# One branch around all of TensorE's rounds, and the output weight's argument on GpSimd, in an RWKV and SwiGLU layer

## The chip, the cores and the metric

The kernel runs on one core of a Trainium2 chip. The metric is the device time of one execution in microseconds (us). The time before is the median of three runs, 326.41 us (324.96 to 333.9). A core has five engines that run their own instruction streams and wait for each other by semaphores: TensorE (PE; its weight loads are PEld), VectorE (DVE), ScalarE (ACT), GpSimd (POOL) and SyncE (SP, which only issues transfers here).

## The reference

The input is `x`, 4096 rows of 256 numbers. The layer is an RWKV attention and a SwiGLU feed-forward, each followed by a residual and a layer norm:

```python
xk = x*mix_k + xx*(1-mix_k)        # xx: x shifted by one row; the same for v and r
k, v, sr = xk@Wk.T, xv@Wv.T, sigmoid(xr@Wr.T)
# per channel, over the rows in order, w = -exp(time_decay), u = time_first
q = max(pp, u+k);  y = (exp(pp-q)*aa + exp(u+k-q)*v) / (exp(pp-q)*bb + exp(u+k-q))
q2 = max(pp+w, k); aa, bb, pp = exp(pp+w-q2)*aa + exp(k-q2)*v, exp(pp+w-q2)*bb + exp(k-q2), q2
x1  = layernorm(x + (sr*y)@Wo.T)
out = layernorm(x1 + (silu(x1@(wg/127).T) * (x1@(wu/127).T)) @ (wd/127).T)
```

`wg`, `wu` and `wd` are int32 matrices (768 hidden columns) with values from -127 to 127.

## The kernel before, in words

The 4096 rows are cut into nine chunks (`NC`): seven of 512 rows, and one of 256 at either end. Channels lie on the partitions, as two halves `h` of 128. Round `j` does the attention of chunk `j`, the feed-forward of chunk `j-1`, and prepares chunks `j+1` and `j+2`. Each engine has its order written out by hand: rounds 0, 1, 2, 7 and 8 stand by themselves, rounds 3 to 6 in a loop (`Fori`), two rounds in a pass on TensorE, ScalarE and GpSimd, one on VectorE. So a loop of TensorE makes two passes.

In a round TensorE computes gate and up of chunk `j-1` (L1012, six tiles of 128 hidden columns), `down` (L1035), then `attention_out` of chunk `j` (L980), the projections K and V of chunk `j+1` (L970), the transposes of `x1` (L989) and the projection R (L970). The matrices of the feed-forward exist in two forms: values that TensorE's fast format (`f32r`) holds exactly, used when all weights are below 4096 in size, and full float32, used when not. Which of the two is decided at run time: a flag `wide` is made by VectorE in round 0 and loaded into a register of TensorE (L1105), and each of the rounds 1 to 8, and the last `ffn_products`, has an `If` with both forms written out (L1060). With the inputs of the reference the first form always runs, and at its end TensorE jumps over the second, to `attention_out`.

The recurrence is done with a running maximum `pmax` (L616) and `gap = k - pmax` (L623). Three exponentials follow for each half of a chunk. Their arguments are made by VectorE in `exp_args` (L633) from `gap`: `IN_NEW` and `IN_OLD` with the decay, and `OUT`, the weight of the current row in the output, as `min(gap + time_first, 30)`. ScalarE takes the exponentials (`weight`, L414). It waits for VectorE's counter `args_ready`, in the order of the arguments. The scans over the rows (L650, L662) begin when all three weights of a half are there.

In a steady round VectorE's order after the scans is: products of gate and up (L758), the low parts of the last two hidden tiles (L766), gating (L696), `divide` (L705, writes `rwkv`), the residual of the feed-forward (L774) and its statistics, the residual of the attention (L725) and its statistics (L712, L717), the running maxima, the gaps, the arguments of half 0, `shift_rows2` (L781), `IN_NEW` and `IN_OLD` of half 1, the low parts of `x1` (L746), `OUT` of half 1, and then the next round's scans.

GpSimd's order in a round is: low parts of four hidden tiles (L348) with the two halves of the numerator (L340) between them, then, once `rwkv` is written, the differences `dx` (L327) and the sums `mix` (L333) of chunk `j+2`. Then it waits for the next round's first hidden tile.

Of the kernel before, what the change touches and what calls it, by code (L numbers as in the profile page):

```python
# [14 lines left out]
def rwkv_swiglu_kernel(nc: bass.Bass, xT: bass.AP, x: bass.AP, params: bass.AP, wk: bass.AP, wv: bass.AP,  # L15
# [4 lines left out]
    ALU = mybir.AluOpType  # L20
# [29 lines left out]
    with ctx:  # L50
# [131 lines left out]
        args_ready = sem("args_ready")  # L182
        wts_ready = sem("wts_ready")
# [138 lines left out]
        def _(pool):  # L322
# [19 lines left out]

            def low_part(c, m):
# [16 lines left out]
            def round_(j, s, ffn, ahead):  # L360
# [11 lines left out]
                if ahead:  # L372
                    pool.wait_ge(rwkv_ready, j + 1)
                    diffs(j + 2)
                    mix_chunk(j + 2, s)

# [4 lines left out]
            for h in range(CH):  # L381
                pool.wait_ge(r0_scaled, h + 1)
                nc.gpsimd.tensor_tensor(mix0[:, R, h, :], mix0[:, R, h, :], xt0[:, h, 0:steps(0)],
                                        ALU.add).then_inc(r0_mixed, 1)
            diffs(1)
            mix_chunk(1, 1)
            pool.wait_ge(wd_in, 16)
            nc.gpsimd.tensor_copy(wd_r[:, :, :], wd_i[:, :, :]).then_inc(wd_ready, 1)
            diffs(2)
# [11 lines left out]
            with pool.Fori(3, NC - 2, 2) as j:  # L401
                round_(j, 1, True, True)
                round_(j + 1, 0, True, True)
# [6 lines left out]
        def _(sc):  # L410
            def weight(c, i, h):
                sc.wait_ge(args_ready, c * (NW * CH) + (h * NW + i + 1))
# [190 lines left out]
        def _(dve):  # L603
# [22 lines left out]
            def exp_args(c, h, which=range(NW)):  # L626
# [4 lines left out]
                for i in which:  # L631
                    s = par[:, FIRST, h:h + 1] if i == OUT else decay[:, h:h + 1]
                    nc.vector.tensor_scalar(wts[:, i, h, 0:n], gap[:, h, 0:n], s, CAP if i == OUT else 0.0, ALU.add,  # L633
# [150 lines left out]
            def round_(j, ffn, nxt):  # L784
# [40 lines left out]
                if first(j):  # L825
# [4 lines left out]
                    exp_args(1, 1, [IN_NEW, IN_OLD])  # L830
                    wide_flag()
                    norm_rows(0, x1, res1, mv1, rstd1, rstd1_ready, x1_ready, halved(0))
                    exp_args(1, 1, [OUT])
# [19 lines left out]
                exp_args(j + 1, 1, (IN_NEW, IN_OLD))  # L853
                x1_low(j, 0)
                x1_low(j, 1)
                exp_args(j + 1, 1, [OUT])
# [82 lines left out]
        def _(pe):  # L939
# [118 lines left out]
            def round_(j, s, ffn, nxt):  # L1058
                if ffn:
                    with pe.If(any_wide == 0):  # L1060
                        ffn_products(j, False)
                    with pe.Else():
                        ffn_products(j, True)
# [45 lines left out]
            round_(1, 0, True, True)  # L1109
            round_(2, 1, True, True)  # L1110
            with pe.Fori(3, NC - 2, 2) as j:
                round_(j, 0, True, True)
                round_(j + 1, 1, True, True)
            round_(NC - 2, 0, True, True)
            round_(NC - 1, 1, True, False)
            with pe.If(any_wide == 0):
                ffn_products(NC, False)
# [30 lines left out]
```

## Time and profile before

| | |
|---|---|
| median of 3 runs | 326.41 us (324.96, 326.41, 333.9) |
| the profiled execution | 325.1 us, of which the span of the instructions is 323.3 us |
| mean granted clock of TensorE | 0.954 of full speed |
| busy share: PE, PEld, DVE, ACT, POOL | 87%, 64%, 84%, 67%, 46% |
| instructions on PE, DVE, ACT, POOL | 1250, 484, 386, 123 |
| the chain that ended last, by engine | DVE 32%, PE 30%, issue 17%, ACT 15%, DMA 3% |

A busy share is an average over the whole span. "Issue" in the chain is time in which an engine waited for nothing that the profile shows. Semaphore, register and branch instructions are not counted as busy. The time of the profiled execution is 1.8 us more than its span.

### The profile page before, as it was taken

The page shows a single profiled execution, that of the slowest core. Times are in us where ns is not written, and L with a number is a line of the kernel's source. Part 1 is how long each engine was busy: PE and PEld are TensorE (multiplying, and loading weights), DVE is VectorE, ACT ScalarE, POOL GpSimd, SP SyncE. Part 2 cuts the span into 40 slices and gives each one's busy share as a digit, 9 for nine tenths or more (in the row PEclk, how much of TensorE's full clock was granted, in tenths as well). Part 3 has the DMA queues.
Part 4 walks back from the last instruction along what each step waited for, and adds up shares of the span by engine and source line. Part 5 has one row for each costly group of instructions (what it writes and reads, how often), then busy time and mean ns, then how long its engine had stood idle before and what let it go on. Part 6 is the DMA issues. An engine that isn't in the chain of part 4 may idle for free.

```text
span 323.3 us, 4411 instructions
## 1 busy us (share of the span) xinstructions
PE 280.9 (87%) x1250; PEld 205.6 (64%) x1250; DVE 272.6 (84%) x484; ACT 218.0 (67%) x386; POOL 148.8 (46%) x123
## 2 busy tenths in 40 slices
PE   7878869908997999599997999999989998999892
PEld 5624756505885468465885568846785588868782
DVE  4999798629985999669986899899989998989664
ACT  3587767069764688529884498569855986299275
POOL 2564255491569019560378208570759056006030
PEclk9979799976997999989997999999999999999998
DMA  7802200402000301012010401020012001101002
GB/s 256 296 0 65 68 1 2 132 0 65 32 3 3 130 3 65 2 30 102 2 65 5 130 0 65 0 74 23 6 58 65 0 1 67 36 0 65 2 6 99
DMA packets 13531, 16.38 MB, mean 51 GB/s; under 512 B 704, under 2 KB 11200, under 8 KB 13504
## 3 DMA queue, kind: packets, MB, share of 16 engines
q1 hardware_dynamic: 12816, 15.48, 14.5%
q10 hardware_dynamic: 688, 0.53, 0.5%
q8 instruction: 18, 0.29, 0.4%
q14 instruction: 9, 0.07, 0.1%
HBM read 11.81 MB, written 4.19 MB: 50 GB/s over the span
## 4 chain that ended last, share of the span: by engine, by line
DVE 32%; PE 30%; issue 17%; ACT 15%; DMA 3%; DVEq 1%; POOL 1%; SPq 0%; ACTq 0%; POOLq 0%
PE bank_b L980 7%; PE bank_b L1012 6%; PE bank_a L1012 6%; DVE hid L758 4%; DVE wts L633 3%; ACT L512 3%; PE bank_c L970 3%; DVE stats L712 3%; DVE pmax L616 3%; DVE state L662 3%; ACT den L452 2%; ACT x L437 2%; ACT den L458 2%; DVE res L725 2%; DVE rwkv L705 2%
## 5 line engine op out<-in xcount | busy, mean ns | idle before, releaser
L348 POOL TENSOR_TENSOR hlo<-hid,hhi 128x512 fp32r<-128x512 f32 (+1 forms) x36 | 47.5, 1321 | 123.2 <-ACT hhi L496 123.2
L333 POOL TENSOR_TENSOR mix<-mix,xt 128x512 f32<-128x512 f32 x48 | 56.7, 1213 | 13.0 <-ACT mix L422 13.0
L1035 PE MATMUL bank_a<-wd_r,hhi 128*128 128x256 f32 x192 | 47.3, 287 | 4.6 <-DVE hlo L766 4.6
L422 ACT ACTIVATE mix<-dx,par 128x512 f32<-128x512 f32 x48 | 31.2, 710 | 27.0 <-POOL dx L327 26.9
L1035 PE MATMUL bank_a<-wd_r,hlo 128*128 128x256 f32 x192 | 45.6, 279 | 0.0
L980 PE MATMUL bank_b<-woT,rwkv 128*128 128x256 f32 x128 | 34.9, 432 | 8.6 <-issue 7.6
L1035 PEld LDWEIGHTS bank_a<-wd_r,hhi 128*128 128x128 f32 x192 | 36.0, 188 | 7.8 <-issue 7.0
L496 ACT ACTIVATE hhi<-hid 128x512 fp32r<-128x512 f32 (+1 forms) x54 | 31.1, 578 | 10.6 <-DVE hid L758 10.6
L980 PEld LDWEIGHTS bank_b<-woT,rwkv 128*128 128x128 f32 x128 | 27.2, 218 | 14.7 <-issue 8.8
L1035 PEld LDWEIGHTS bank_a<-wd_r,hlo 128*128 128x128 f32 x192 | 36.0, 188 | 0.3 <-issue 0.2
L414 ACT ACTIVATE wts<-wts 128x512 f32<-128x512 f32 (+1 forms) x54 | 27.9, 578 | 8.3 <-DVE wts L633 8.3
L1012 PE MATMUL bank_a<-x1hi,wg_r 128*128 128x512 f32 (+1 forms) x96 | 31.9, 412 | 1.6 <-ACT act L488 1.0
L488 ACT ACTIVATE act<-bank_a 128x512 f32<-128x512 f32 (+1 forms) x48 | 27.3, 568 | 6.6 <-PE bank_a L1012 6.1
L758 DVE TENSOR_TENSOR hid<-bank_b,act 128x512 f32<-128x512 f32 (+1 forms) x48 | 30.6, 642 | 1.3 <-PE bank_b L1012 0.8
L970 PE MATMUL bank_d<-mix,wvT 128*128 128x512 f32 (+1 forms) x64 | 28.9, 596 | 2.3 <-POOL mix L333 2.3
L1012 PE MATMUL bank_b<-x1hi,wu_r 128*128 128x512 f32 (+1 forms) x96 | 29.2, 385 | 1.6 <-DVE hid L758 1.6
L1012 PE MATMUL bank_a<-x1lo,wg_r 128*128 128x512 f32 (+1 forms) x96 | 29.0, 382 | 0.1
L1012 PE MATMUL bank_b<-x1lo,wu_r 128*128 128x512 f32 (+1 forms) x96 | 28.8, 381 | 0.0
L970 PE MATMUL bank_c<-mix,wrT 128*128 128x512 f32 (+1 forms) x64 | 28.7, 591 | 0.0
L327 POOL TENSOR_TENSOR dx<-xt 128x512 f32<-128x512 f32 x16 | 16.5, 1054 | 25.3 <-DVE rwkv L705 16.1
L970 PE MATMUL bank_a<-mix,wkT 128*128 128x512 f32 (+1 forms) x64 | 27.2, 567 | 1.1 <-POOL mix L333 1.1
L472 ACT ACTIVATE lnv<-mv,eps 128x4 f32<-128x4 f32 (+1 forms) x18 | 5.2, 289 | 30.5 <-DVE mv L717 30.5
(103 smaller groups left out, 571.7 us busy)
## 6 DMA issues: line engine op xcount, KB each, us to landing
xt<-xT SPq DMA_DIRECT2D x7, 513.0 KB, 4.7
xrow<-x SPq DMA_DIRECT2D x7, 512.0 KB, 3.8
out<-y SPq DMA_DIRECT2D x6, 512.0 KB, 2.8
wg_i<-wg SPq DMA_DIRECT2D x1, 768.0 KB, 7.7
wu_i<-wu SPq DMA_DIRECT2D x1, 768.0 KB, 9.1
wd_i<-wd SPq DMA_DIRECT2D x1, 768.0 KB, 10.4
out<-y SPq DMA_DIRECT2D x3, 256.0 KB, 2.1
xt<-xT SPq DMA_DIRECT2D x2, 257.0 KB, 3.0
```

The costliest lines, as they stand in the source:

```text
L327: nc.gpsimd.tensor_tensor(dx[:, h, 0:n], xt[:, h, 1:n + 1], xt[:, h, 0:n], ALU.subtract).then_inc(dx_ready, 1)
L333: nc.gpsimd.tensor_tensor(mix[:, s, i, h, 0:n], mix[:, s, i, h, 0:n], xt[:, h, 0:n], ALU.add).then_inc(mixed, 1)
L348: nc.gpsimd.tensor_tensor(hlo[:, m, 0:n], hid[:, m % NH, 0:n], hhi[:, m, 0:n].bitcast(f32), ALU.subtract).then_inc(hlo_ready, 1)
L414: nc.scalar.activation(wts[:, i, h, 0:n], wts[:, i, h, 0:n], ACT.Exp, scale=-1.0 if i == IN_OLD else 1.0).then_inc(wts_ready, 1)
L422: nc.scalar.activation(mix[:, s, i, h, 0:n], dx[:, h, 0:n], ACT.Copy, scale=par[:, MIX + i, h:h + 1]).then_inc(dx_scaled, 1)
L488: nc.scalar.activation(act[:, m % 2, 0:n], gate_bank(c)[:, m % 2, 0:n], ACT.Silu, scale=SCALE).then_inc(act_ready, 1)
L496: nc.scalar.activation(hhi[:, m, 0:n], hid[:, m % NH, 0:n], ACT.Copy).then_inc(hhi_ready, 1)
L758: nc.vector.tensor_tensor(hid[:, m % NH, 0:n], up_bank(c)[:, m % 2, 0:n], act[:, m % 2, 0:n], ALU.mult).then_inc(hid_ready, 1)
L970: mm = nc.tensor.matmul(bank[:, d, 0:n], w[:, h, d * P:(d + 1) * P], mixed_x[:, i, h, 0:n], start=(h == 0), stop=(h == CH - 1))
L980: mm = nc.tensor.matmul(attn[:, q, :], rwkv[:, h, q * P:(q + 1) * P], woT[:, h, :], start=(h == 0), stop=(h == CH - 1))
L1012: mm = nc.tensor.matmul(bank[:, m % 2, 0:steps(c)], w[:, h, m * P:(m + 1) * P], xp, start=(h == 0 and part is x1hi), stop=(h == CH - 1 and ...
L1035: mm = nc.tensor.matmul(ffn[:, q, :], hp.bitcast(f32) if full else hp, w[:, m, :], start=(m == 0 and q % 2 == 0 and part is hhi), stop=(m ...
```

## The change

Three things are changed.

TensorE: the `If` on `any_wide` no longer stands in each round but once, around everything from round 1 to the end, with the whole sequence of rounds (and its loop) written out in either branch.

The `OUT` argument is made by GpSimd, in a new function `out_arg`, with a semaphore of its own; VectorE's `exp_args` makes only `IN_NEW` and `IN_OLD`. ScalarE's order of the exponentials is the same; for `OUT` it waits for the new semaphore.

GpSimd: the loop over rounds 3 to 6 is written out as four rounds.

```diff
+            def out_arg(c, h):
+                pool.wait_ge(gap_ready, c * CH + (h + 1))
+                n = steps(c)
+                nc.gpsimd.tensor_scalar(wts[:, OUT, h, 0:n], gap[:, h, 0:n], par[:, FIRST, h:h + 1], CAP, ALU.add,
+                                        ALU.min).then_inc(out_arg_ready, 1)
...
                     mix_chunk(j + 2, s)
+                if not last(j):
+                    out_arg(j + 1, 0)
+                    out_arg(j + 1, 1)
...
+            pool.wait_ge(par_in, 16)
+            out_arg(0, 0)
             diffs(1)
+            out_arg(0, 1)
             mix_chunk(1, 1)
             pool.wait_ge(wd_in, 16)
             nc.gpsimd.tensor_copy(wd_r[:, :, :], wd_i[:, :, :]).then_inc(wd_ready, 1)
+            out_arg(1, 0)
+            out_arg(1, 1)
             diffs(2)
...
-            with pool.Fori(3, NC - 2, 2) as j:
-                round_(j, 1, True, True)
-                round_(j + 1, 0, True, True)
+            for j in range(3, NC - 2):
+                round_(j, j % 2, True, True)
...
             def weight(c, i, h):
-                sc.wait_ge(args_ready, c * (NW * CH) + (h * NW + i + 1))
+                if i == OUT:
+                    sc.wait_ge(out_arg_ready, c * CH + (h + 1))
+                else:
+                    sc.wait_ge(args_ready, c * (2 * CH) + (h * 2 + i + 1))
...
-            def exp_args(c, h, which=range(NW)):
+            def exp_args(c, h):
...
-                for i in which:
-                    s = par[:, FIRST, h:h + 1] if i == OUT else decay[:, h:h + 1]
-                    nc.vector.tensor_scalar(wts[:, i, h, 0:n], gap[:, h, 0:n], s, CAP if i == OUT else 0.0, ALU.add,
+                for i in (IN_NEW, IN_OLD):
+                    nc.vector.tensor_scalar(wts[:, i, h, 0:n], gap[:, h, 0:n], decay[:, h:h + 1], 0.0, ALU.add,
                                             ALU.max if i == IN_OLD else ALU.min).then_inc(args_ready, 1)
...
-                exp_args(j + 1, 1, (IN_NEW, IN_OLD))
+                exp_args(j + 1, 1)
                 x1_low(j, 0)
                 x1_low(j, 1)
-                exp_args(j + 1, 1, [OUT])
...
-            def round_(j, s, ffn, nxt):
+            def round_(j, s, ffn, nxt, full=False):
                 if ffn:
-                    with pe.If(any_wide == 0):
-                        ffn_products(j, False)
-                    with pe.Else():
-                        ffn_products(j, True)
+                    ffn_products(j, full)
...
+            def rounds(full):
+                round_(1, 0, True, True, full)
+                round_(2, 1, True, True, full)
+                with pe.Fori(3, NC - 2, 2) as j:
+                    round_(j, 0, True, True, full)
+                    round_(j + 1, 1, True, True, full)
+                round_(NC - 2, 0, True, True, full)
+                round_(NC - 1, 1, True, False, full)
+                ffn_products(NC, full)
+
             with pe.If(any_wide == 0):
-                ffn_products(NC, False)
+                rounds(False)
             with pe.Else():
-                ffn_products(NC, True)
+                rounds(True)
```

How the instructions stand in a row shows at three places. First TensorE in round 2, from the last products of `down` to `attention_out`, before (the names `wg_r`, `wd_r` are the exact form, `wg_i`, `wd_i` the full float32 form):

```order
L1035 MATMUL bank_a<-wd_r,hlo 128x256
L1060 UNCONDITIONAL_BRANCH
L1012 MATMUL bank_a<-x1hi,wg_i 128x512 x2
L1012 MATMUL bank_a<-x1lo,wg_i 128x512 x2
...
L1035 MATMUL bank_a<-wd_i,hlo 128x256
L1062 UNCONDITIONAL_BRANCH
L980 MATMUL bank_b<-woT,rwkv 128x256 x8
L970 MATMUL bank_a<-mix,wkT 128x512 x4
```

The same place with the change:

```order
L1049 MATMUL bank_a<-wd_r,hhi 128x256
L1049 MATMUL bank_a<-wd_r,hlo 128x256
L1049 MATMUL bank_a<-wd_r,hhi 128x256
L1049 MATMUL bank_a<-wd_r,hlo 128x256
L994 MATMUL bank_b<-woT,rwkv 128x256 x8
L984 MATMUL bank_a<-mix,wkT 128x512 x4
L984 MATMUL bank_d<-mix,wvT 128x512 x4
```

The second form no longer lies between `down` and `attention_out`, and no branch is there.

Second, GpSimd at the end of the loop's first round and the start of its second, before (`ISA` and `REGISTER_ALU` set the values that a wait compares with):

```order
L331 REGISTER_ALU
L333 TENSOR_TENSOR mix<-mix,xt 128x512
L344 ISA
L348 TENSOR_TENSOR hlo<-hid,hhi 128x512
L344 REGISTER_ALU
L348 TENSOR_TENSOR hlo<-hid,hhi 128x512
L344 REGISTER_ALU
L348 TENSOR_TENSOR hlo<-hid,hhi 128x512
```

And with the change, at the end of a round and the start of the next:

```order
L328 TENSOR_TENSOR dx<-xt 128x512 x2
L334 TENSOR_TENSOR mix<-mix,xt 128x512 x6
L347 TENSOR_SCALAR wts<-gap,par 128x512 x2
L355 TENSOR_TENSOR hlo<-hid,hhi 128x512 x3
L341 TENSOR_TENSOR num<-kv,state 128x512
```

The two arguments of `OUT` stand behind the sums of `mix` and ahead of the next round's low parts.

Third, VectorE at the end of a steady round, from the gaps on, before:

```order
L623 TENSOR_TENSOR gap<-bank_a,pmax 128x512 x2
L633 TENSOR_SCALAR wts<-gap,decay 128x512 x2
L633 TENSOR_SCALAR wts<-gap,par 128x512
L781 SCALAR_TENSOR_TENSOR shift<-mv,rstd 128x4
L633 TENSOR_SCALAR wts<-gap,decay 128x512 x2
L746 TENSOR_TENSOR x1lo<-bank_b,x1hi 128x512 x2
L633 TENSOR_SCALAR wts<-gap,par 128x512
```

And with the change:

```order
L640 TENSOR_TENSOR gap<-bank_a,pmax 128x512 x2
L649 TENSOR_SCALAR wts<-gap,decay 128x512 x2
L797 SCALAR_TENSOR_TENSOR shift<-mv,rstd 128x4
L649 TENSOR_SCALAR wts<-gap,decay 128x512 x2
L762 TENSOR_TENSOR x1lo<-bank_b,x1hi 128x512 x2
```

One instruction between the pairs of arguments is gone, and one behind the low parts of `x1`.

## Rows read from the trace of the kernel before

**Rows 1.** Windows between `rwkv`s: start:end, length, busy PE PEld DVE ACT POOL, PEclk, DMA, GB/s.
```profile
95.48:132.25 36.77, 33.68 (x144) 24.36 (x144) 31.38 (x55) 25.34 (x43) 18.15 (x14) 0.95 0.13 45
132.25:169.48 37.23, 33.76 (x144) 24.33 (x144) 31.19 (x56) 25.35 (x43) 18.04 (x14) 0.95 0.14 44
169.48:206.34 36.86, 33.77 (x144) 24.33 (x144) 31.39 (x55) 25.33 (x43) 18.12 (x14) 0.95 0.13 44
206.34:240.03 33.69, 32.12 (x144) 22.90 (x144) 31.87 (x56) 25.11 (x43) 18.57 (x14) 1.00 0.13 39
240.03:273.69 33.66, 32.21 (x144) 23.04 (x144) 32.02 (x56) 25.10 (x43) 18.54 (x14) 1.00 0.10 32
```

**Rows 2.** The chain that ended last: its pieces between `down` and `attention_out` (start, us, what).
```profile
96.86 2.38 issue
...
133.66 2.85 issue
...
170.89 2.39 issue
...
305.40 1.10 issue
```

**Rows 3.** Timeline of PE: `attention_out` of rounds 4 and 5 (start, us, instruction, idle before).
```profile
173.28 5.40 PE L980 MATMUL bank_b<-woT,rwkv 128*128 128x256 f32 x16 [2.39 <-issue]
...
207.69 3.72 PE L980 MATMUL bank_b<-woT,rwkv 128*128 128x256 f32 x16
```

**Rows 4.** The window of round 4's `attention_out`, same columns as the windows above.
```profile
173.28:178.68 5.40, 5.40 (x17) 4.48 (x18) 1.44 (x3) 2.82 (x5) 5.40 (x6) 0.68 0.02 5
```

**Rows 5.** DMA queues from 95 to 105 us: packets, MB, share.
```profile
q8 instruction: 2, 0.03, 1.3%
```

**Rows 6.** DMA queues from 175 to 260 us, the only queue with packets.
```profile
q1 hardware_dynamic: 3184, 3.41, 12.7%
```

**Rows 7.** Timeline of VectorE and ScalarE at the end of round 5.
```profile
217.73 1.25 DVE L623 TENSOR_TENSOR gap<-bank_a,pmax 128x512 f32<-128x512 f32 x2
218.91 0.86 DVE L633 TENSOR_SCALAR wts<-gap,decay 128x512 f32<-128x512 f32 x2
219.70 0.47 DVE L633 TENSOR_SCALAR wts<-gap,par 128x512 f32<-128x512 f32 x1
220.10 0.15 DVE L781 SCALAR_TENSOR_TENSOR shift<-mv,rstd 128x4 f32<-128x4 f32 x1
...
221.08 1.29 DVE L746 TENSOR_TENSOR x1lo<-bank_b,x1hi 128x512 fp32r<-128x512 f32 x2
222.29 0.48 DVE L633 TENSOR_SCALAR wts<-gap,par 128x512 f32<-128x512 f32 x1
...
221.43 2.19 ACT L414 ACTIVATE wts<-wts 128x512 f32<-128x512 f32 x4
```

**Rows 8.** Timeline of GpSimd: the next round's first low part, and its idle time before.
```profile
228.01 1.46 POOL L348 TENSOR_TENSOR hlo<-hid,hhi 128x512 fp32r<-128x512 f32 x1 [11.41 <-ACT hhi L496]
```

**Rows 9.** Groups on GpSimd, shapes apart: count | busy us, mean ns of one.
```profile
L340 POOL TENSOR_TENSOR num<-kv,state 128x512 f32<-128x512 f32 x14 | 25.4, 1811 | 0.0
L327 POOL TENSOR_TENSOR dx<-xt 128x512 f32<-128x512 f32 x16 | 16.5, 1054 | 25.3 <-DVE rwkv L705 16.1 <-DMA xt<-xT 9.2
L388 POOL CAST wd_r<-wd_i 128x1536 fp32r<-128x1536 int32 x1 | 1.5, 1460 | 0.0
L379 POOL TENSOR_SCALAR_AFFINE_SELECT ident<-ident 128x128 f32<-128x128 f32 x1 | 0.3, 292 | 0.2 <-POOL ident L377 0.2
```

**Rows 10.** Timeline of the first 30 us: arguments on VectorE beside work on GpSimd.
```profile
13.48 1.18 DVE L633 TENSOR_SCALAR wts<-gap,par 128x256 f32<-128x256 f32 x1
28.28 2.32 POOL L327 TENSOR_TENSOR dx<-xt 128x512 f32<-128x512 f32 x2 [2.50 <-DMA xt<-xT]
29.62 1.26 DVE L633 TENSOR_SCALAR wts<-gap,par 128x512 f32<-128x512 f32 x1
```

**Rows 11.** Timeline of VectorE in the last round: the rows that TensorE transposes.
```profile
305.28 0.74 DVE L732 TENSOR_SCALAR xt<-res,mv,rstd 128x256 f32<-128x256 f32 x2 [0.67 <-ACT rstd L474]
```

More of the change, by code:

```diff
@@ L182, in rwkv_swiglu_kernel @@
         args_ready = sem("args_ready")
+        out_arg_ready = sem("out_arg_ready")
         wts_ready = sem("wts_ready")
@@ L829, in round_ @@
                     range_flag()
-                    exp_args(1, 1, [IN_NEW, IN_OLD])
+                    exp_args(1, 1)
                     wide_flag()
                     norm_rows(0, x1, res1, mv1, rstd1, rstd1_ready, x1_ready, halved(0))
-                    exp_args(1, 1, [OUT])
                     x1_low(0, 0)
@@ L1108, in _ @@
             pe.wait_ge(wd_ready, 1)
[L1109 to L1115, printed above, removed]
+            def rounds(full):
[7 more added lines that the diff above has]
+                ffn_products(NC, full)
             with pe.If(any_wide == 0):
-                ffn_products(NC, False)
+                rounds(False)
             with pe.Else():
-                ffn_products(NC, True)
+                rounds(True)
 def kernel(**inputs):
```

## The prediction

> **What bounds the kernel now.** I cut the span into windows first, from one `rwkv` to the next, for rounds 2 to 7 [rows 1]. Three periods take 36.77, 37.23 and 36.86 us, the next two 33.69 and 33.66 us, with the same counts of matmuls. A round can therefore run in 33.7 us, and three do not: 3.09 + 3.55 + 3.18 = 9.8 us more.
>
> The chain of waits says where. In each of the three, TensorE has a piece of "issue" between the last product of `down` and `attention_out`: 2.38, 2.85 and 2.39 us, and one of 1.10 us in the last round [rows 2]. `rwkv` had been written before that time was over, so no data were missing. In round 5 the same 16 matmuls follow `down` at once [rows 3]. The second effect is the clock: they take 5.40 us behind the pause and 3.72 us without it [rows 3], at a granted clock of 0.68 [rows 4] against 1.00 in the whole of that round [rows 1]. Pause and slow clock make TensorE 2.4 + 1.7 = 4.1 us late. Of that VectorE, which has the feed-forward's residual to do meanwhile, hides 0.9; 3.2 us stay in the period.
>
> What stands at this place in the program is the jump over the full float32 form. The queues support it: from 95 to 105 us, around the first pause, the instruction queue q8 moves two packets [rows 5]; from 175 to 260 us, the loop's second pass and a little more, only the data queue moves anything [rows 6]. I read the pause as the fetch of code at a jump's target that is not at hand.
>
> In an undisturbed round VectorE bounds: 31.9 of 33.7 us busy [rows 1], and dense from the gaps into the scans [rows 7].
>
> **The change, part by part.** *The branch.* It removes the jump from rounds 1 to 8 and the pause with it. Rounds 2, 3 and 4 should take what 5 and 6 take: 9.8 us less. What is late next is what bounds rounds 5 and 6 already, so this is not an extrapolation. The order shows no second copy of the products in TensorE's path any more. One jump over the whole second sequence remains, behind all of TensorE's work, where VectorE's last norm and the store end the kernel: nothing. The loop's jump back stays; before, it cost nothing, since round 5 needed no fetch [rows 6] though its body held both forms. Now it is shorter.
>
> *The last round.* The 1.10 us piece goes [rows 2]. Four warming matmuls and the transposes behind it move forward; their input comes from VectorE, at 305.28 + 0.74 = 306.02 [rows 11], 0.5 us before the pause's end, and the warming matmuls run ahead of it. I take 1.0 us, bounds 0.5 and 1.1.
>
> *`OUT` off VectorE.* Two instructions per steady round go, at 219.70 and 222.29 [rows 7]. Each occupies VectorE for 0.40 us, the step from 219.70 to the next one's start at 220.10. The first gains nothing ahead of `x1`'s low parts, which start just when ScalarE has written their input; the second is directly ahead of the next scans and gains 0.4.
>
> *`OUT` on GpSimd.* The trace has no such instruction. GpSimd has done its sums at 228.01 - 11.41 = 216.6 and is then idle until the next round's first low part [rows 8], so its own time is covered; ScalarE takes `OUT` of half 0 only at 221.43 [rows 7], 3 us after its gap. The price is paid by VectorE. Beside work of GpSimd one argument took 1.18 us (256 wide) and 1.26 us (512 wide) [rows 10] against 0.47 alone [rows 7]: it ended 0.28 us after GpSimd's instruction did, so it had waited for it. Now GpSimd starts on half 0 at about 218.5, exactly when VectorE comes to its arguments. Call one such instruction D. The nearest rows: the cast, one input, 1460/1536 = 0.95 ns an element, so 0.49 us and some 0.2 us of fixed time for 512 elements (an affine select of 128 takes 0.29); two inputs take 1.05 us, contended 1.81 [rows 9]. I take D = 0.7, by the row with one input; ends 0.5 and 1.8. With 0.7: GpSimd 218.5 to 219.2, VectorE's first argument until 219.6, GpSimd's half 1 until 220.3, VectorE's second until 220.7, against 219.70 before. The next pair and `shift_rows2` follow at 220.7, and the low parts start at 221.5 instead of 221.08: +0.45, less the 0.40 behind them. That is +0.05 us a round, and 2(D - 0.7) more for another D. Over seven rounds: +0.3, taken as 0, with ends -2.5 (D = 0.5) and +15.7 (D = 1.8).
>
> The Trainium skill gives a lower price (GPSIMD Engine Reference, section "Elementwise — side-by-side cycle accounting": a loop with one or two operations runs at about 1.03 cycles an element), an estimate of 0.44 us for 512 elements; by it the seven rounds would give back some 3 us rather than nothing, and the time would be near 310.5. No run here shows it.
>
> *The start.* VectorE is the chain up to 25 us. The two `OUT` instructions of 1.18 and 1.26 us there [rows 10] go, 2.4 us; but GpSimd now waits for a gap ahead of `dx`, and the collisions shift rather than vanish. I take 1.5, bounds 0 and 2.8 (with the two shorter ones of half 0). It survives: the load of chunk 3 waits for a residual of round 1 and moves along.
>
> *GpSimd's loop written out.* It is idle for 11 us of a round; nothing.
>
> **Sum.** 9.8 + 1.0 + 1.5 + 0 = 12.3 us. Against the profiled execution (325.1 us, of which 323.3 is the span) that gives 312.8. That execution lies between the lowest and the middle run of three; the median is 1.3 us above it, so the same sum against the median gives 314.1. I say 313.5.
>
> **The rivals.**
> *A. The stall moves.* The rows do not say why the jumps of rounds 1 and 7 cost nothing, so how much code is at hand is inferred. If TensorE's jump back to round 5 misses now, one period pays 3.2 us again: 316.7. Against it stands that the second pass needed no fetch [rows 6]. Chance 0.08. The Trainium skill speaks for this rival (Runtime: NRT & Kernel Launch, section "Instruction fetch mechanics": only two blocks of code are held, and a taken branch outside them stalls); by that rule the second pass before should have fetched too, and the trace disagrees, with no packet on q8 in 85 us.
> *B. The port eats it.* D near 1.3, as with two inputs: 7 x 2 x 0.6 = 8.4 us, giving 321.9. For it: GpSimd's arithmetic in this trace is never under 1.05 us at this width. Against: one input only. Chance 0.10; at about D = 1.1 the result passes from "faster by 2%" to "within 2%".
> *C. The change doesn't do what it says:* the pause belongs not to the jump but to `attention_out` itself, and stays. Only 1.5 us come: 325. Against: round 5 has no pause at the same instruction. Chance 0.05.
> *D. Slower.* GpSimd needs 2.3 us or more for this form (a minimum behind an addition with a per-partition operand, which no row shows). VectorE's arguments then wait for two such instructions in every round: 7 x 3.2 = 22 us, and the start's 1.5 are lost: 337.5. It decides from D = 2.1 on. Against: the longest arithmetic of this width, contended, is 1.8 us on average [rows 9]. Chance 0.03.
>
> **The numbers.** The forecast has 0.74. Its own range goes from 325.1 - 9.8 - 1.1 - 2.8 - 2.5 = 308.9 to 318 (nothing at the start, D = 0.9). With A and most of B inside, the range is 308.5 to 321. This kernel's measurement tells 2%, 6.5 us, from no change: faster means below 319.9. Faster: 0.74 + 0.08 + half of B (0.04) = 0.86. Within 2%: rest of B, and C, 0.11. Slower: 0.03.
>
> **What would show it.** All periods near 33.7 us, no "issue" ahead of `attention_out`, its 16 matmuls at 3.7 us with the clock at full speed in every round. GpSimd's new instruction at about 0.7 us, right behind the gaps; VectorE's first two arguments stretched to about 1.8 us together, scans no later than before. In the last round, transposes 1 us sooner. It is wrong if a pause stands at another place of TensorE's stream, if D is over 1.1 us, or if rounds 5 and 6 are themselves longer than 34.5 us.

## The result and the profile after

The changed kernel takes 311.18 us (median of 4 runs, 310.65 to 311.65). Of the kernel before there were then four runs, 324.96, 326.41, 333.9 and one of 458.12. The ratio of the times, taken with the first two of these, is 0.9554, with a 95% interval of 0.9509 to 0.9599: 4.5% faster. The profiled execution took 311.22 us (span 309.4) against 325.1 (span 323.3): 13.9 us less. The forecast was 313.5 us, with 12.3 us for the profiled execution.

The windows of the changed kernel from one `rwkv` to the next come first, rounds 1 to 6 of it; columns as in [rows 1], which hold rounds 2 to 6:

```profile
51.72:93.51 41.79, 30.64 (x134) 22.33 (x132) 29.40 (x47) 26.59 (x45) 28.33 (x20) 0.88 0.13 45
93.51:126.17 32.66, 31.94 (x144) 23.16 (x144) 31.14 (x54) 25.31 (x43) 22.61 (x16) 1.00 0.16 49
126.17:159.86 33.69, 32.22 (x144) 22.91 (x144) 31.82 (x53) 25.20 (x43) 22.90 (x16) 1.00 0.15 48
159.86:193.56 33.70, 32.40 (x144) 23.05 (x144) 31.83 (x53) 25.21 (x43) 22.90 (x16) 1.00 0.16 47
193.56:227.25 33.69, 32.40 (x144) 23.08 (x144) 31.81 (x53) 25.21 (x43) 22.92 (x16) 1.00 0.13 39
227.25:259.81 32.56, 31.94 (x144) 23.15 (x144) 30.90 (x53) 25.23 (x43) 18.61 (x16) 1.00 0.10 33
```

The three long periods of [rows 1] are 4.11, 3.54 and 3.16 us shorter, 10.8 together; the fourth is as before (33.69); the fifth is 1.0 shorter (its end in [rows 1] was read 0.08 us late: `rwkv` of round 7 starts at 273.61, so it was 33.58). `rwkv` of round 1 is written at 51.72 instead of 54.20, and the period after it is 0.5 longer (41.79 for 41.28). From the last `rwkv` to the end nothing changes (23.35 us for 23.47). 2.5 - 0.5 + 10.8 + 1.0 + 0.1 are the 13.9 us.

TensorE's `attention_out` of round 5 (timeline; start, us, instruction), and the instruction queue over the whole span, first of the kernel before, then of the changed one:

```profile
194.92 3.72 PE L994 MATMUL bank_b<-woT,rwkv 128*128 128x256 f32 x16
```

```profile
q8 instruction: 18, 0.29, 0.4%
```

```profile
q8 instruction: 10, 0.16, 0.2%
```

No idle time stands ahead of the 16 matmuls in any of the rounds 2 to 6, and the clock is at full speed in all their periods (PEclk 1.00 above, where [rows 1] had 0.95 three times). So both effects that [rows 3] and [rows 4] show, the pause and the slow clock behind it, are gone.

The end of round 5 on VectorE, GpSimd and ScalarE, which answers to [rows 7] and [rows 8]:

```profile
204.86 1.25 DVE L640 TENSOR_TENSOR gap<-bank_a,pmax 128x512 f32<-128x512 f32 x2
205.62 4.43 POOL L347 TENSOR_SCALAR wts<-gap,par 128x512 f32<-128x512 f32 x2 [1.89 <-DVE gap L640]
...
206.04 0.94 DVE L649 TENSOR_SCALAR wts<-gap,decay 128x512 f32<-128x512 f32 x2
...
206.97 1.22 DVE L649 TENSOR_SCALAR wts<-gap,decay 128x512 f32<-128x512 f32 x2
208.28 1.29 DVE L762 TENSOR_TENSOR x1lo<-bank_b,x1hi 128x512 fp32r<-128x512 f32 x2
208.62 2.18 ACT L431 ACTIVATE wts<-wts 128x512 f32<-128x512 f32 x4
209.49 0.58 DVE L659 COPY state<-state 128x4 f32<-128x4 f32 x1
```

One argument takes GpSimd 2.2 us, not 0.7. And yet VectorE is hardly held: its four arguments take 0.94 and 1.22 us where they took 0.86 and 0.87, the copy of the state 0.58 where it took 0.16. That is 0.85 us more, about what the two instructions taken from it gave (0.8). ScalarE gets the last argument at 205.62 + 4.43 = 210.05, and the last of its four exponentials begins at 210.2: the margin is 0.2 us.

### The profile page after: what moved, and what is told of

It is laid out like the page before. It is cut to its first block, busy times and chain, and to the rows that moved or that the text cites. A ratio compares the mean times of both kernels' runs of the same rounds, so it can differ in the third digit from the quotient of the medians.

```text
span 309.4 us, 4331 instructions
## 1 busy us (share of the span) xinstructions
PE 273.7 (88%) x1250; PEld 199.5 (64%) x1250; DVE 267.7 (87%) x466; ACT 217.7 (70%) x386; POOL 181.9 (59%) x141
## 4 chain that ended last, share of the span: by engine, by line
PE 41%; DVE 22%; ACT 17%; issue 10%; POOL 4%; DMA 2%; DVEq 1%; SPq 0%; ACTq 0%; POOLq 0%
PE bank_a L1026 10%; PE bank_b L1026 10%; PE bank_c L984 7%; PE bank_b L994 4%; ACT L529 3%; DVE stats L728 3%; ACT x L454 3%; ACT den L469 3%; ACT den L475 3%; PE bank_b L1003 2%; DVE rwkv L721 2%; PE bank_d L984 2%; PE bank_a L984 2%; POOL wts L347 2%; DVE hid L774 2%
## 5 line engine op out<-in xcount | busy, mean ns | idle before, releaser
L355 POOL TENSOR_TENSOR hlo<-hid,hhi 128x512 fp32r<-128x512 f32 (+1 forms) x36 | 50.3, 1399 | 59.6 <-ACT hhi L513 59.5
L334 POOL TENSOR_TENSOR mix<-mix,xt 128x512 f32<-128x512 f32 (+1 forms) x48 | 53.5, 1148 | 6.6 <-ACT mix L439 6.6
L347 POOL TENSOR_SCALAR wts<-gap,par 128x512 f32<-128x512 f32 (+1 forms) x18 | 35.4, 1968 | 25.5 <-DVE gap L640 24.6
L984 PE MATMUL bank_a<-mix,wkT 128*128 128x512 f32 (+1 forms) x64 | 30.0, 615 | 5.3 <-POOL mix L334 5.3
L994 PE MATMUL bank_b<-woT,rwkv 128*128 128x256 f32 x128 | 29.9, 385 | 0.9 <-DVE rwkv L721 0.9
L328 POOL TENSOR_TENSOR dx<-xt 128x512 f32<-128x512 f32 (+1 forms) x16 | 15.7, 1001 | 21.7 <-DVE rwkv L721 15.7
L994 PEld LDWEIGHTS bank_b<-woT,rwkv 128*128 128x128 f32 x128 | 23.7, 190 | 5.4 <-DVE rwkv L721 1.4
L984 PE MATMUL bank_d<-mix,wvT 128*128 128x512 f32 (+1 forms) x64 | 27.1, 566 | 0.0
```

Of the source, the lines that this page charges most:

```text
L334: nc.gpsimd.tensor_tensor(mix[:, s, i, h, 0:n], mix[:, s, i, h, 0:n], xt[:, h, 0:n], ALU.add).then_inc(mixed, 1)
L347: nc.gpsimd.tensor_scalar(wts[:, OUT, h, 0:n], gap[:, h, 0:n], par[:, FIRST, h:h + 1], CAP, ALU.add, ALU.min).then_inc(out_arg_ready, 1)
L355: nc.gpsimd.tensor_tensor(hlo[:, m, 0:n], hid[:, m % NH, 0:n], hhi[:, m, 0:n].bitcast(f32), ALU.subtract).then_inc(hlo_ready, 1)
L984: mm = nc.tensor.matmul(bank[:, d, 0:n], w[:, h, d * P:(d + 1) * P], mixed_x[:, i, h, 0:n], start=(h == 0), stop=(h == CH - 1))
L994: mm = nc.tensor.matmul(attn[:, q, :], rwkv[:, h, q * P:(q + 1) * P], woT[:, h, :], start=(h == 0), stop=(h == CH - 1))
```

## The experiments

The references for all are the changed kernel (311.18 us) and the kernel before. A ratio is to the kernel before as it ran beside the experiment, with its 95% interval. The median of the kernel before was then 329.6, 331.4 and 326.6 us, while the runs of each other kernel lie within 3 us; so I compare the kernels' own medians, and periods. A "profiled" time is that of the one run whose trace is read.

### The branch alone

`rounds(full)` and the single `If` as in the change; VectorE's and GpSimd's parts as before.

> Only TensorE's branch is moved around all rounds; VectorE makes all three arguments and GpSimd has its loop, as before. Theory: the jump was the cause of the pauses. Rounds 3, 4 and 5 (from one rwkv to the next) fall from 36.8 to 37.2 us to 33.7 (or 32.7 where VectorE's carry of the maximum slips between two instructions of GpSimd), nothing else changes, the start least of all: rwkv of round 1 at 54.2 us as before, period 6 to 7 at 33.7. Profiled time 325.1 - 9.8 = 315.3 us, to 314 if one period gives 1 us more. Rival (the pause belongs to attention_out, and what the change gained came from the argument moved): time near 325, pauses of 2.4 us stay.

314.6 us (313.63 to 315.03), ratio 0.9546 (0.9465 to 0.9628); profiled 314.68. Its windows for rounds 1 to 4 and 6:

```profile
54.11:95.67 41.56, 30.75 (x134) 22.39 (x132) 30.70 (x50) 26.84 (x45) 23.15 (x18) 0.88 0.14 45
95.67:128.32 32.65, 31.95 (x144) 23.16 (x144) 31.18 (x55) 25.34 (x43) 18.15 (x14) 1.00 0.16 49
128.32:162.00 33.68, 32.30 (x144) 23.05 (x144) 31.86 (x55) 25.12 (x43) 18.55 (x14) 1.00 0.16 47
162.00:195.70 33.70, 32.30 (x144) 23.05 (x144) 31.87 (x55) 25.13 (x43) 18.48 (x14) 1.00 0.15 47
...
229.40:263.04 33.64, 32.23 (x144) 23.07 (x144) 31.99 (x56) 25.13 (x43) 18.59 (x14) 1.00 0.11 31
```

The steady periods are those of the changed kernel to 0.02 us, with VectorE's two instructions still in place. The branch gave all of the gain there. Of the other 3.5 us of the change, most lie in the start (54.11 for 51.72) and in round 6 (33.64 for 32.56).

### The argument alone

```diff
-                    ffn_products(j, full)
+                    with pe.If(any_wide == 0):
+                        ffn_products(j, False)
+                    with pe.Else():
+                        ffn_products(j, True)
...
-                rounds(False)
+                ffn_products(NC, False)
```

The changed kernel with TensorE's branch back in every round.

> Only the output weight's argument is moved to GpSimd, with GpSimd's loop over rounds 3 to 6 written out; TensorE keeps its branch in every round. Theory: the pauses stay in rounds 2, 3 and 4 (2.4 to 2.9 us each). The start gains the 2.5 us that rwkv of round 1 gained in the changed kernel, less 0.5 in the next period; steady rounds are within 0.1 us of before, although one argument takes GpSimd 2.2 us; the round before chunk 8 gains 1.1 from the loop written out. 325.1 - 2.0 - 1.1 = 322.0 us, bounds 321 and 324. Rival (GpSimd's 2.2 us block VectorE's arguments, and it was the branch that paid for that): steady rounds longer by 1 us or more, the time 325 or above.

325.67 us (324.44 to 327.27), ratio 0.9895 (0.9805 to 0.9985): above the expected bounds (321 to 324) and within the rival's "325 or above", but not by the rival's cause, since no steady round became longer. The start and round 6 gained as expected. What was not expected is on TensorE's weight loads (timeline, last bracket the idle time before):

```profile
170.29 1.98 PEld L994 LDWEIGHTS bank_b<-woT,rwkv 128*128 128x128 f32 x7 [2.58 <-issue]
...
273.59 0.50 PEld L994 LDWEIGHTS bank_b<-woT,rwkv 128*128 128x128 f32 x2 [2.88 <-issue]
```

A fourth pause stands in round 7, with the same instructions on TensorE as before, and makes the period to the last `rwkv` 30.5 us instead of 26.2. The instruction queue shows what differs. Here a packet of code stands at 271.0 us, just behind the last product of `down` (it begins at 270.6). In the kernel before one stands at 271.2, when `down` still waited for VectorE, until 273.8, for its last eight products, and no pause followed. Why it comes earlier there with the same instructions stays open. Round 5, which has no pause, takes 33.70 us, as without the move.

The pause in round 2 parts the two effects, pause and clock (timeline of TensorE, and the window of these matmuls):

```profile
97.63 3.69 PE L994 MATMUL bank_b<-woT,rwkv 128*128 128x256 f32 x16 [2.51 <-issue]
```

```profile
97.63:101.32 3.69, 3.69 (x17) 3.28 (x18) 1.45 (x3) 2.62 (x5) 3.69 (x4) 1.00 0.02 4
```

The clock did not fall behind this pause, and the period is 35.47 us, where the next two, with clocks of 0.70 and 0.68 in the same 16 matmuls, take 37.33 and 36.75. And that although its copy of the carry took 1.02 us, where theirs took 0.17.

### No distance, and the jump at another place

First the kernel before without the full float32 form, which these inputs never take:

```diff
                     with pe.If(any_wide == 0):
                         ffn_products(j, False)
-                    with pe.Else():
-                        ffn_products(j, True)
...
```

The `Else` of the last `ffn_products` goes too.

> The kernel before, with the branch in each round, but without the full float32 form: nothing stands in the Else (left out is the form for weights of 4096 and more, which these inputs never take). Theory (the pause is the fetch of code at a jump's target that is not at hand): compare and branch remain, the distance is gone, so the pauses go too: no issue ahead of attention_out, periods 3, 4 and 5 at 33.7 or 32.7 us, the time that of the branch-only kernel, 314.6 (profiled 314 to 316). Rival (branching itself costs, whatever its distance): pauses of 2.4 us stay in rounds 2, 3 and 4, time near 325.

313.16 us (312.94 to 313.28), ratio 0.943 (0.9358 to 0.9501). Its first three long periods are 32.63, 33.69 and 33.69 us. Nine compares and branches remain and cost nothing that can be seen; it is the distance that cost. The 1.4 us less than with one branch stand at the end: from the last `rwkv` to the end of the span it is 22.15 us here and 23.54 there (see the experiment on the end of the span).

Then the kernel before with the forms exchanged, here and in the last `ffn_products`, so that the jump stands at the round's start:

```diff
-                    with pe.If(any_wide == 0):
-                        ffn_products(j, False)
+                    with pe.If(any_wide == 1):
+                        ffn_products(j, True)
                     with pe.Else():
-                        ffn_products(j, True)
+                        ffn_products(j, False)
```

> The kernel before with the two forms exchanged in the text: the full float32 form stands first and is jumped over at the round's start, ahead of gate and up; behind down nothing is jumped over. The distance is the same. Theory: the fetch is needed as often, but it now falls where the 8 matmuls of the projection R (3.4 us) have already been handed to TensorE, which works on them while the code comes. So no pause is seen ahead of attention_out, and at most 0.5 us ahead of gate and up: 315 to 317 us. Rival (a pause costs the same wherever it stands): a piece of issue of about 2.4 us ahead of the first gate product in three rounds, time 322 to 326.

314.43 us (312.27 to 315.08), ratio 0.9453 (0.9372 to 0.9534): about the time with one branch, by the exchange of two blocks of text. It is not free throughout: `rwkv` of round 1 comes 0.7 us later than with one branch, and rounds 1 and 2 are 0.4 us longer each, while the end, which here has no jump, is 1.4 us shorter. The queue fetches as often as before. The page's line on it, the longest idle time of the weight loads ahead of a gate product, and the windows of rounds 2 and 3:

```profile
q8 instruction: 18, 0.29, 0.4%
```

```profile
113.04 0.30 PEld L1012 LDWEIGHTS bank_a<-x1hi,wg_r 128*128 128x128 f32 x2 [0.94 <-issue]
```

```profile
96.77:129.79 33.02, 32.20 (x144) 23.05 (x144) 31.54 (x56) 25.33 (x43) 18.15 (x14) 1.00 0.16 49
129.79:163.47 33.68, 32.30 (x144) 22.95 (x144) 31.86 (x56) 25.11 (x43) 18.55 (x14) 1.00 0.17 48
```

18 packets, and 0.94 us of idle time once on the weight loads (0.1 us on the matmuls). What was 2.4 to 2.9 us behind `down` is hidden behind the projection R, as the times of the packets show:

```profile
109.34 3.60 PE L970 MATMUL bank_c<-mix,wrT 128*128 128x512 f32 x8
113.05 0.73 PE L1012 MATMUL bank_a<-x1hi,wg_r 128*128 128x512 f32 x2
```

The round's packet is at 110.1 us, and the gate product comes 2.9 us later, while the 3.6 us of matmuls run. In the kernel before the packets of rounds 2, 3 and 4 are at 96.6, 133.4 and 170.7, within 0.3 us of the last product of `down`, and `attention_out` follows 2.6, 3.1 and 2.6 us later with nothing in between. My bound of 0.5 us held for the matmuls, not for the weight loads.

### GpSimd's loop written out

```diff
-            with pool.Fori(3, NC - 2, 2) as j:
-                round_(j, 1, True, True)
-                round_(j + 1, 0, True, True)
+            for j in range(3, NC - 2):
+                round_(j, j % 2, True, True)
```

The branch alone, and this.

> The branch moved, and GpSimd's loop written out, with all arguments on VectorE. It differs from the kernel with the branch alone only in GpSimd's loop. Theory: written out, round 6 knows that chunk 8 has 256 rows, so the differences and sums for it take 256 columns instead of 512: GpSimd's sums end some 3 us earlier there, before VectorE copies the carried maximum, which then takes 0.2 us instead of 1.0. Period 6 to 7 falls from 33.7 to 32.6 us, all others as with the branch alone: 1.1 us less than that kernel. Rival (a written-out loop costs or gives nothing but code): no period changes, the same time as the branch alone.

The sums of `mix` for chunk 8, first in the kernel with the branch alone, then written out:

```profile
232.78 6.88 POOL L333 TENSOR_TENSOR mix<-mix,xt 128x512 f32<-128x512 f32 x6
```

```profile
232.99 3.90 POOL L333 TENSOR_TENSOR mix<-mix,xt 128x256 f32<-128x256 f32 x6 [0.26 <-ACT mix L421]
```

In the loop the chunk's number is a register, and `steps(c)` gives 512 for the last chunk too. Written out, it gives 256, the period falls from 33.64 to 32.56 us, and no other steady period moves by more than 0.1. The time does not show it: 314.34 us (313.94 to 314.78) against 314.6, where 1.1 less was expected. In this kernel's profile `rwkv` of round 1 was 1.3 us later (55.38 for 54.11), with the same code there; of its other runs there is no trace.

### What the GpSimd instruction costs, and whom

The changed kernel with each argument made twice:

```diff
+                nc.gpsimd.tensor_scalar(spare[:, 0:n], gap[:, h, 0:n], par[:, FIRST, h:h + 1], CAP, ALU.add,
+                                        ALU.min).then_inc(spare_ready, 1)
+                pool.wait_ge(spare_ready, c * CH + (h + 1))
```

> The changed kernel, in which GpSimd makes each of its arguments twice, first into a spare tile, then where it belongs, so 9 us of such instructions in a steady round instead of 4.4. Theory (GpSimd's instruction does not hold VectorE for its length; only short overlaps cost): VectorE's arguments and scans lengthen by under 0.5 us a round, but ScalarE takes OUT of half 0 some 2 us late and of half 1 4 us late, and the scans wait for that: 2 to 4 us a round, time 325 to 338. What tells the theories apart is the length of VectorE's four arguments: 2.2 us together now. Rival (the port is held for the whole instruction): they stretch to 4 us or more.

341.43 us (340.55 to 341.93), ratio 1.0279 (1.0199 to 1.0359), 30 us more than the changed kernel; the steady period is 37.59 us, 3.9 more. The end of its round 5, VectorE and ScalarE:

```profile
228.08 0.94 DVE L654 TENSOR_SCALAR wts<-gap,decay 128x512 f32<-128x512 f32 x2
...
229.01 1.22 DVE L654 TENSOR_SCALAR wts<-gap,decay 128x512 f32<-128x512 f32 x2
...
236.29 0.63 ACT L436 ACTIVATE wts<-wts 128x512 f32<-128x512 f32 x1 [2.50 <-POOL wts L352]
...
236.95 1.28 DVE L671 TENSOR_TENSOR_SCAN state<-wts,state 128x512 f32<-128x512 f32 x1 [2.31 <-ACT wts L436]
```

VectorE's arguments take the same 0.94 and 1.22 us with GpSimd busy beside them all the time: it is not held for an instruction's length. The loss is the plain wait: ScalarE for the argument, VectorE's scan for ScalarE. The expected 325 to 338 us were too few, since the start (6.4 us) and round 1 (4.0) pay too.

To see what makes it slow, the argument was replaced (the output weight is then not the reference's): half 0 is one operation with the per-partition operand, half 1 two operations with constants.

```diff
+                if h == 0:
+                    nc.gpsimd.tensor_scalar(wts[:, OUT, h, 0:n], gap[:, h, 0:n], par[:, FIRST, h:h + 1], None,
+                                            ALU.min).then_inc(out_arg_ready, 1)
+                else:
+                    nc.gpsimd.tensor_scalar(wts[:, OUT, h, 0:n], gap[:, h, 0:n], 0.5, CAP, ALU.add,
+                                            ALU.min).then_inc(out_arg_ready, 1)
```

> The changed kernel with other arguments for the output weight, so that GpSimd's time for them can be told apart (the weight computed is not the reference's): half 0 is one operation, a minimum with the per-partition operand; half 1 is two operations, an addition and a minimum, with constants. In the changed kernel both operations with the per-partition operand take 2.0 us uncontended, where the forecast took 0.7. Theory 1: the second operation costs, so half 0 takes 0.6 to 0.8 us and half 1 about 2.0. Theory 2: the per-partition operand costs, so half 0 takes about 2 and half 1 0.7. Theory 3: both halves take 1.5 to 2.0, the instruction is slow in any form. The time changes by under 1 us in all of them, 310 to 311.5.

Groups on GpSimd (count | busy us, mean ns of one):

```profile
L351 POOL TENSOR_SCALAR wts<-gap 128x512 f32<-128x512 f32 x7 | 13.8, 1970 | 0.6
L348 POOL TENSOR_SCALAR wts<-gap,par 128x512 f32<-128x512 f32 x7 | 12.5, 1787 | 11.4 <-DVE gap L644 11.4
```

1.97 and 1.79 us: neither the second operation nor the operand alone makes the difference to the forecast's 0.7 us. Theory 3 held; one operation with a constant was not run. The time is that of a single run, 309.6 us.

### The end of the span

The changed kernel with the two sequences exchanged (`If(any_wide == 1): rounds(True)`, `Else: rounds(False)`), so that TensorE jumps at the start and falls through at the end.

> The changed kernel with the two sequences of rounds exchanged: TensorE jumps over the full float32 sequence at the start of round 1 and falls through at the end. Theory: the changed kernel loses 1.2 us at its end (3.3 us from the last store's issue to the end of the span, 2.1 before) because TensorE's last jump fetches blocks of code on the same DMA engines as the last store; with the exchange this comes back, and one fetch of 2.4 us stands ahead of round 1's gate products, where the warming matmuls hide part: 310.5 us, bounds 309 and 312.5. Rival (the end of the span varies for another reason): 3.3 us at the end stay, time 311 to 313.5.

311.03 us (310.55 to 311.51), ratio 0.9372 (0.9301 to 0.9444) against a slower set of runs of before, so no different from 311.18. The issue of the last store, before, changed, exchanged (spans 323.3, 309.4 and 308.6 us):

```profile
320.84 0.37 SPq L287 DMA_DIRECT2D out<-mix  x1
```

```profile
305.72 0.37 SPq L288 DMA_DIRECT2D out<-mix  x1
```

```profile
306.18 0.37 SPq L288 DMA_DIRECT2D out<-mix  x1
```

From that issue's end to the end of the span: 2.1, 3.3 and 2.0 us. So the changed kernel's last jump costs 1.2 us at the very end, and the exchange takes it back. All traces agree: the eight in which TensorE jumps over the whole second sequence at its end have one packet of code in the last 5 us of the span and 2.8 to 3.8 us from the store's issue to the end; the other six have no such packet and 2.0 to 2.1 us. In the changed kernel the packet is at 305.2 us, half a microsecond ahead of the store. That the two share a DMA engine is likely, but was not shown.

The jump at the start does not come for nothing: TensorE's first gate product of round 1 is 3.5 us late behind it (it begins at 40.16, with 3.50 us of idle time before it), but these products wait for other engines later, and `rwkv` of round 1 comes only 0.7 us later (52.44 for 51.72).

### What holds VectorE: a small copy

The periods of 32.6 and 33.7 us differ in one instruction. The carry of the running maximum (2 elements a partition) in rounds 2 and 5 of the changed kernel:

```profile
100.17 0.22 DVE L625 COPY pmax<-pmax 128x2 f32<-128x2 f32 x1
...
200.49 1.00 DVE L625 COPY pmax<-pmax 128x2 f32<-128x2 f32 x1
```

In round 5 the copy ends at 201.49, with the GpSimd sum that runs from 200.36 to 201.46; in round 2 it starts 0.2 us before the end of one. The statistics behind it lead to `x1`. The kernel before has both too, in a long round (4) and in a short one (5):

```profile
180.24 0.17 DVE L608 COPY pmax<-pmax 128x2 f32<-128x2 f32 x1
...
213.26 1.09 DVE L608 COPY pmax<-pmax 128x2 f32<-128x2 f32 x1
```

In round 4 GpSimd had done its sums at 179.71, since the pause of TensorE holds VectorE up and not GpSimd; in round 5 they last to 216.60. The edit:

```diff
-                nc.vector.tensor_copy(pmax[:, :, 0:1], pmax[:, :, n:n + 1]).then_inc(pmax_carried, 1)
+                nc.vector.tensor_reduce(pmax[:, :, 0], pmax[:, :, n:n + 1], mybir.AxisListType.X,
+                                        ALU.max).then_inc(pmax_carried, 1)
```

> The changed kernel, with one instruction of VectorE in another form: the last column of the running maximum is carried by a reduction over one element instead of a copy. Theory: in steady rounds this copy (1.0 us for 2 elements a partition; 0.17 to 0.22 where GpSimd is idle or between two instructions) waits for GpSimd's sum that runs beside it, and it lies on the chain to x1, since the statistics are aggregated behind it; a reduction is not held. Periods 3 to 6 fall from 33.7 us to about 32.8, those of 2 to 3 and 6 to 7 (32.7, 32.6) stay; 3 x 0.85 = 2.6 us less, 308.6 against 311.2. Rival 1: the wait passes to the next instruction on the ports, shift_rows1 (two inputs in SBUF), and the time stays. Rival 2: the reduction waits as well: same durations as the copy.

308.11 us (306.81 to 309.33), ratio 0.9344 (0.9258 to 0.943). The same place, and the windows of rounds 3 to 5:

```profile
199.07 0.16 DVE L625 TENSOR_REDUCE pmax<-pmax 128x2 f32<-128x2 f32 x1
```

```profile
126.84:159.49 32.65, 32.02 (x144) 23.17 (x144) 30.80 (x53) 25.35 (x43) 22.41 (x16) 1.00 0.16 49
159.49:192.15 32.66, 32.02 (x144) 23.16 (x144) 30.81 (x54) 25.34 (x43) 22.44 (x16) 1.00 0.16 49
192.15:224.80 32.65, 32.01 (x144) 23.18 (x144) 30.81 (x53) 25.34 (x43) 22.44 (x16) 1.00 0.13 40
```

All steady periods are now 32.6 to 32.7 us, and TensorE is busy for 32.0 of them. The Trainium skill (SBUF — State Buffer, section "Who interferes with whom") states both halves of this: a VectorE `copy` can take a form that uses the ports shared with GpSimd, and `tensor_reduce` on trn2 never contends. The rows agree, 1.00 us against 0.16. The same section says that the one who comes first holds the ports for its whole instruction; beside GpSimd's two-input sums and differences that fits [rows 10], beside its one-input argument it does not (0.94 us for two arguments, within 4.4 us of such instructions).

With the carry of the state in the same form too:

> The changed kernel with both carries of VectorE, of the running maximum and of the scans' state, by a reduction over one element. It differs from the kernel with the first one alone in the second. Theory: the copy of the state takes 0.58 us beside GpSimd's argument and 0.16 alone; as a reduction it takes 0.2, and the scans start 0.4 us sooner, since half 0's weights are there by then. If VectorE's scans and products bound the round, each of six periods falls by up to 0.4: 305.5 to 307 us against 308.1. Rival: ScalarE's last weight of half 1, which ends with GpSimd's second argument, or TensorE's unbroken chain from the residual to the last hidden tile bounds, and nothing changes: 307.5 to 308.5.

306.83 us (306.31 to 308.35), ratio 0.9393 (0.9311 to 0.9475). The steady periods stay at 32.63 to 32.65 us, so the rival held there; the 1.3 us to the kernel with one reduction are in the start and within the two kernels' spread.

And with the branch, the written-out loop and the first reduction, but all arguments on VectorE:

> The branch moved, GpSimd's loop written out, the maximum carried by a reduction, but all arguments on VectorE. It differs from the kernel with the first reduction in the argument's engine alone. Theory: the argument's move pays in the start (rwkv of round 1 at 54.1 instead of 51.7 to 52.8) and gives nothing in steady rounds, because VectorE's gain of 0.8 us is spent on overlaps with GpSimd's 4.4 us: periods 32.65 us as there, time 309.5 to 311 against 308.1. Rival (the move is worth something in every round once the copy no longer hides it): periods of 33.0 to 33.4, time 312 to 314.

306.92 us (305.41 to 307.78), ratio 0.9371 (0.929 to 0.9452). Periods of 32.61 to 32.66 us, and `rwkv` of round 1 at 51.94, where I expected 54.1. In the steady rounds the argument's move is thus worth nothing, as in the experiment with the branch alone. In the start the case is open. Six profiles with the arguments on VectorE and the carry as a copy have `rwkv` of round 1 at 54.1 to 55.4 us, three with the argument moved at 51.7 to 52.4, so the move's gain there is more than chance. This kernel reaches 51.94 without it. Its carry there takes 0.14 us instead of 1.05, which is not 2.2; and the changed kernel did not gain in its start by the same edit (52.77 for 51.72). It is one profile, and what made its start short was not shown.

### The kernel before once more

> The kernel before once more, unchanged, for a second profile. Its runs range from 325 to 334 us, those of all kernels without jumps over the long form by 1 us or less. Theory: whether a jump pauses TensorE is decided in each run by whether the code has arrived, so pauses stand ahead of other attention_outs than in the first profile, or there are more: each one more or less makes 3 to 4 us. In the kernel with only the argument moved one appeared in round 7 (2.7 us, period 30.5 instead of 26.2), where the first profile had none, with the same code on TensorE. A time near 330 should show four or five pauses. Rival: the same three pauses, and the time differs elsewhere.

325.26 us profiled, a second run 330.79. The profile shows the same three pauses, 2.81, 2.70 and 2.94 us on the weight loads, in the same rounds. No trace was taken of a run near 330 us, so whether more pauses make it longer stays open; the fourth pause of the kernel with the argument alone is the only sign.

## Why the prediction was right, and where it was not

- **The jump as the cause of the pauses**: right. Without distance (313.16 us) and with one branch (314.6) they are gone; with the distance at another place (314.43) the code is fetched as often, and no pause stands ahead of `attention_out` or of the gate products of the steady rounds. Rival C is out; rival A too, the second pass through the loop stays at 33.7 us.
- **9.8 us for three rounds**: 10.8. The periods became those of rounds 5 and 6, one of them 1.0 better, because in round 2 VectorE's carry came just before the end of a sum on GpSimd (0.22 us instead of 1.0).
- **"VectorE hides 0.9 us" of the 4.1**: wrong as a mechanism, and without harm to the sum, since both periods of the difference were measured. The 0.9 us are VectorE's copy of the carry, 0.17 us in the long rounds and 1.09 and 1.07 in the short ones. They are not hidden in the long rounds but added in the short ones: against 32.65 us, the period once the carry is a reduction, the three were 4.1, 4.6 and 4.2 us too long, and pause and slow clock come to 4.0, 4.5 and 4.1.
- **The last round, 1.0 us**: the gate products of chunk 8 start 7.2 us after the last `rwkv` instead of 8.6, so TensorE gained 1.4. The end of the span gave back 1.2: the one jump that remains is over the whole second sequence, and "nothing" was the wrong price for it.
- **The start, 1.5 us**: 2.5 - 0.5 = 2.0, inside its bounds. One kernel without the move had as short a start, so the cause is not settled.
- **GpSimd's loop written out, nothing**: wrong by 1.0 to 1.1 us. I looked at the branch and the idle time, and not at what `steps(c)` gives for a register. The order of the two kernels shows the narrower instructions.
- **The argument on GpSimd, 0 us with D = 0.7**: the sum's term was right and both of its parts wrong. D is 2.2 us (2.16 on average), beyond my upper end of 1.8, beyond the point at which rival D was to decide, and beyond the 1.1 us that I had named as a sign of being wrong. The formula with it gives 0.05 + 2 x 1.46 = 3.0 us a round, 21 us in all; the trace shows no change. That the term came out at 0 is luck. The failed step is the transfer of [rows 10]: there VectorE was held by two-input instructions, and I took the hold as that of any instruction. The Trainium skill's price (an estimate of 0.44 us, GPSIMD Engine Reference, section "Elementwise — side-by-side cycle accounting") is further off than mine. What the length does set is when ScalarE gets its argument, which I wrote off as 3 us early; 0.2 us were left.
- The sum, 12.3 us, was 13.9. Its errors are +1.0 (the rounds), +0.5 (the start), +1.0 (the loop) and -0.9 (the end), so part of the agreement is that they cancel.

The best kernels here, at 306.8 to 306.9 us, have the branch moved, the loop written out and the carry reduced. They are 4.3 us below the changed kernel.

## What to carry to other kernels

Cut a kernel with rounds into equal periods first: where equal work takes two different times, the shorter one is a forecast, and the difference names its place; look also for what only the shorter ones pay. A jump over much code cost here what its engine had not queued when it jumped: with 3.6 us of matmuls queued it was nearly free, behind a wait it showed in full, and the clock mostly fell with it. So try to exchange the two arms before rewriting the control flow. The price of contention is that of the pair of instructions that meet, not of one engine's length; measure the pair, and look at small copies that lie on the chain.

## What the runs showed of the hardware

- Nine of the ten pauses of 2.4 to 3.1 us of TensorE ahead of `attention_out` in three traces (the kernel before, its repeat, the argument alone) are followed by a granted clock of 0.68 to 0.71 in its 16 matmuls, which then take 5.2 to 5.4 us instead of 3.7; behind one of 2.51 us the clock stayed at 1.00.
- From the packet of code to the first instruction behind the jump it took 2.6 to 3.1 us (the kernel before, rounds 2 to 4).
- A one-input `tensor_scalar` on GpSimd, 512 float32 wide, takes 1.8 us with one operation and 2.0 to 2.2 with two, more than its two-input difference (1.05 us), and a cast of three times the width takes 1.46 us.
- VectorE's copy of 2 elements a partition takes 0.17 to 1.28 us by what GpSimd runs beside it; the reduction 0.14 to 0.16.
- Nine branches on TensorE instead of one cannot be seen in the steady periods when their targets are near (32.63 and 33.69 us against 32.65 and 33.68).
- A store of 256 KB at the end of the span took 3.3 us from its issue to its landing with one packet of code beside it, 2.1 without.
